# Setup of a graph-attention layer written into the layer's first units, and its residual formed on TensorE

## The reference, cut to what matters

```python
def _L0_gnn_ref(inputs, adj, W, a, bias, res_w, res_b):
    h = inputs @ W
    hr = h.reshape(N, F_OUT, H)
    s_src = jnp.einsum('nfh,fh->nh', hr, a[:F_OUT])
    s_dst = jnp.einsum('nfh,fh->nh', hr, a[F_OUT:])
    e = s_src[:, None, :] + s_dst[None, :, :]
    e = jnp.where(e >= 0, e, ALPHA * e)
    att = jax.nn.softmax(e * adj[:, :, None], axis=1)
    out = jnp.einsum('ijh,jfh->ihf', att, hr)
    out = out.reshape(N, H * F_OUT)
    out = out + bias
    out = out + inputs @ res_w + res_b
    return out
...
x = _layernorm(x + _L0_gnn_ref(x, adj, ...), axis=-1)
x = _layernorm(x + _L1_gnn_ref(x, adj, ...), axis=-1)
```

## Time and profile before

| | |
|---|---|
| median of 3 runs | 4077.73 us |
| profiled execution | 4075.24 us |
| its span in the profile | 4073.3 us |
| first `ex` of layer 0 starts | 137.03 us |
| last `ex` of layer 0 starts | 1542.88 us |
| TensorE, VectorE, ScalarE busy (share of the span) | 90%, 88%, 75% |

### The profile page before, as it was taken

How to read it: one execution, slowest core, us unless ns; L and a number is a source line. 1 busy time by engine, 2 the same in 40 slices (tenths; PEclk the granted TensorE clock), 3 DMA queues, 4 the chain that set the end, 5 groups by cost and what they waited for, 6 DMA issues and landing times.

```text
span 4073.3 us, 66286 instructions
## 1 busy us (share of the span) xinstructions
PE 3664.9 (90%) x25304; PEld 3075.6 (76%) x25304; DVE 3599.6 (88%) x6302; ACT 3068.7 (75%) x3075; POOL 1336.9 (33%) x1508
## 2 busy tenths in 40 slices
PE   7688888888888886999999979999999999999994
PEld 5577777777777774788787858888888788888883
DVE  2899999999999995999999779999999899999994
ACT  3699999899899985555555458888888788888870
POOL 0000000000000000111111035555555469999996
PEclk8899999999999997999999999999999999999997
DMA  3211121121121114000000142333333333333331
GB/s 111 98 54 54 60 74 54 54 79 55 54 72 62 54 54 129 19 17 19 18 17 21 28 142 90 101 101 102 102 102 101 117 111 114 117 117 116 116 109 40
DMA packets 160174, 311.37 MB, mean 76 GB/s; under 512 B 17642, under 2 KB 122346, under 8 KB 155346
## 3 DMA queue, kind: packets, MB, share of 16 engines
q1 hardware_dynamic: 159826, 306.88, 23.1%
HBM read 260.87 MB, written 45.94 MB: 75 GB/s over the span
## 4 chain that ended last, share of the span: by engine, by line
ACT 32%; POOL 20%; DVE 17%; PE 15%; issue 14%; DMA 1%; DVEq 0%; SPq 0%; ACTq 0%; POOLq 0%; PEldq 0%; PEld 0%
ACT b L1008 8%; PE ps L791 7%; ACT b L1144 6%; ACT b L1145 6%; ACT b L1001 5%; DVE b L1349 4%; DVE b L1516 3%; POOL b L585 2%; DVE b L1407 2%; POOL b L582 2%; DVE b L1405 2%; PE ps L747 2%; ACT b L1125 2%; PE ps L932 2%; POOL b L579 2%
## 5 line engine op out<-in xcount | busy, mean ns | idle before, releaser
L859 PE MATMUL ps<-b 128*128 128x257 f32 x4096 | 911.2, 382 | 20.7 <-DMA b<-in_adjTb 11.7
L932 PE MATMUL ps<-b 128*128 128x257 f32 x4096 | 903.0, 380 | 0.0
L859 PEld LDWEIGHTS ps<-b 128*128 128x128 f32 x4096 | 776.8, 190 | 146.1 <-DMA b<-in_adjTb 12.7
L932 PEld LDWEIGHTS ps<-b 128*128 128x128 f32 x4096 | 772.0, 190 | 113.4 <-ACT b L1082 0.8
L791 PE MATMUL ps<-cb,b 128*128 128x128 f32 x4096 | 566.3, 298 | 250.5 <-ACT b L1001 236.9
L791 PEld LDWEIGHTS ps<-cb,b 128*128 128x128 f32 x4096 | 506.3, 154 | 303.6 <-ACT b L1001 245.5
L1296 DVE SCALAR_TENSOR_TENSOR b<-b 128x4096 f32<-128x4096 f32 x128 | 566.5, 4425 | 60.9 <-ACT b L995 58.3
L1298 DVE CUSTOM_DVE_ANT_0 b<-b 128x4096 f32<-128x4096 f32 x128 | 566.4, 4425 | 5.4 <-DMA b<-in_adj 1.0
L548 POOL TENSOR_TENSOR cb<-cb 128x1 f32<-128x1 f32 x32 | 39.4, 1230 | 1521.9 <-DVE cb L1282 1521.9
L1008 ACT ACTIVATE b<-ps 128x1024 f32<-128x1024 f32 x512 | 493.6, 1023 | 45.9 <-PE ps L791 45.5
L747 PE MATMUL ps<-b 128*64 128x128 f32 x8192 | 510.3, 276 | 0.0
(11 more groups left out here) (192 smaller groups left out, 4877.6 us busy)
## 6 DMA issues: line engine op xcount, KB each, us to landing
b<-in_adjTb SPq DMA_DIRECT2D x256, 512.0 KB, 3.7
b<-in_adj SPq DMA_DIRECT2D x32, 2048.0 KB, 8.3
y_d<-b SPq DMA_DIRECT2D x64, 128.0 KB, 1.8
h_d<-b SPq DMA_DIRECT2D x64, 128.0 KB, 1.8
b<-h_d SPq DMA_DIRECT2D x64, 128.0 KB, 2.5
b<-in_xT SPq DMA_DIRECT2D x1, 4096.0 KB, 16.4
b<-in_x SPq DMA_DIRECT2D x32, 128.0 KB, 2.1
b<-y_d SPq DMA_DIRECT2D x32, 128.0 KB, 2.0
```

Source lines behind the costliest of these rows:

```text
L859: last = mm(b[:, 0:XA], aj[:, q % AJR, e, :], xf[:, j, :], start=(j == 0), stop=(j == NT - 1))
L932: last = mm(o[:, 0:XA], at[:, q % ATR, b, :], xa[:, j, :], start=(j == 0), stop=(j == NT - 1))
```

## The change

The ring `pt` has 4 buffers where it had 5; the buffers of the setup are laid over buffers that layer 0 uses later (xT over the second adjacency buffer and `pt`, `hr` over `ub[2]`). The barrier `kA` is gone, and each user waits for the semaphore of what it needs. xT is loaded in four quarters, each with a semaphore of its own, and the adjacency of tile 0 right behind. ScalarE's and TensorE's setup steps are interleaved: two tiles of features follow each broadcast from the fifth on (`groups`), and `linear(0)`, `linear(1)`, `ex(0)`, `ex(1)` and `linear(2)` stand between them.

The x @ res_w tile, its bias sum on VectorE and the tensor `y0_d` are gone. VectorE adds the identity to res_w once, so that x @ (res_w + I) is residual and input together, and adds the two biases once. In `turn_back(t)` TensorE forms identity x bias plus x @ (res_w + I) for the tile in the upper half of the PSUM bank; SyncE loads the tile's columns of xT for it (`xtl`). ScalarE copies the result to `ys` in a new step `ev_y0`, behind `ex` of the units with h = 1, and `post_a` waits for that copy.

```diff
-    PTR = 5
+    PTR = 4
...
+        groups = {i: (2 * (i - NL // 2) + 1, 2 * (i - NL // 2) + 2) for i in range(NL // 2, 2 * NL)}
+        groups[2 * NL] = tuple(range(3 * NL + 1, NT))
...
-            ld(xT_s, xT.rearrange("(k p) n -> p k n", p=128), s_x0)
+            for q in range(4):
+                w = slice(q * N // 4, (q + 1) * N // 4)
+                ld(xT_s[:, :, w], xT[:, w].rearrange("(k p) n -> p k n", p=128), s_x0[q])
...
-                    ld(ys[:, r % 2, :], tile_of(y0_d, r), s_y0l[r % 2])
+                    if r >= 1:
+                        sp.wait_ge(s_of, r)
+                    ld(xtl, xT[:, r * 128:(r + 1) * 128].rearrange("(k p) n -> p k n", p=128), s_xtl)
...
             def turn_back(t):
                 pe.wait_ge(s_ot, t + 1)
+                pe.wait_ge(s_xtl, 16 * (t + 1))
+                y = bank(6 + t % 2)[:, 256:512]
+                mm(y, ident_s, bb, start=True, stop=False)
+                for k in range(2):
+                    mm(y, xtl[:, k, :], RW[:, k, :], start=False, stop=(k == 1))
...
+            def ev_y0(t):
+                ac.wait_ge(s_of, t + 1)
+                if t >= 2:
+                    ac.wait_ge(s_t, xslot[t - 2] + 1)
+                    ac.wait_ge(s_yd[t % 2], 16 * (t // 2))
+                act(ys[:, t % 2, :], bank(6 + t % 2)[:, 256:512], ACT.Copy).then_inc(s_yv, 1)
...
-            linear(0)
-            linear(1)
+            features_ev(0)
+            for i in range(NL // 2):
+                broadcast_ev(i)
+            linear(0)
...
+            for i in range(NL // 2, 2 * NL):
+                broadcast_ev(i)
+                for t in groups[i]:
+                    features_ev(t)
+                if i == NL - 1:
+                    linear(1)
+                if i == NL + 2:
+                    ex(0)
+                if i == 2 * NL - 1:
+                    ex(1)
+                    linear(2)
+            for t in groups[2 * NL]:
+                features_ev(t)
             for u in range(NU):
-                ex(u)
+                if u >= 2:
+                    ex(u)
+                if u % 4 == 1 and u >= 5:
+                    ev_y0(u // 4 - 1)
...
             def post_a(t):
-                ve.wait_ge(s_of, t + 1)
-                ve.wait_ge(s_y0l[t % 2], 16 * (t // 2 + 1))
+                ve.wait_ge(s_yv, t + 1)
```

More of the change, by code:

```diff
@@ L132, in gat_topp_kernel @@
         WD = p0.take(2, 40)
[L133 to L138, removed]
+        bb2 = p0.take(256)
         w1s = p0.take(256)
@@ L231, in gat_topp_kernel @@
         s_c = sem("s_c")
-        s_x0 = sem("s_x0")
-        s_xi = [sem(f"s_xi{i}") for i in range(4)]
-        s_y0 = [sem(f"s_y0{i}") for i in range(4)]
+        s_x0 = [sem(f"s_x0{i}") for i in range(4)]
+        s_rw = sem("s_rw")
+        s_bb = sem("s_bb")
+        s_rwi = sem("s_rwi")
+        s_xtl = sem("s_xtl")
+        s_gw = sem("s_gw")
+        s_mc = sem("s_mc")
+        s_yv = sem("s_yv")
         s_ms = sem("s_ms")
@@ L250, in gat_topp_kernel @@
         s_adj = [sem(f"s_adj{i}") for i in range(2)]
-        s_y0l = [sem(f"s_y0l{i}") for i in range(2)]
         s_gu = sem("s_gu")
@@ L348, in _ @@
[L348 to L351, removed]
+            ld(adj_s[0], tile_of(adj, 0), s_adj[0])
+            ld(ident_s, ident, s_rw)
+            ld(RW, res_w.rearrange("(k p) n -> p k n", p=128), s_rw)
+            ld(bb, bias.partition_broadcast(128), s_rw)
+            ld(bb2, res_b.partition_broadcast(128), s_rw)
@@ L699, in _ @@
             last.then_inc(s_wa, 1)
[L700 to L704, removed]
             pe.wait_ge(s_wab, 1)
-            pe.wait_ge(s_x0, 16)
             for c in range(NL):
+                pe.wait_ge(s_x0[4 * c // NL], 16)
                 if c >= 2:
@@ L713, in _, with broadcast @@
                 last.then_inc(s_sr, 1)
-            pe.wait_ge(s_lo, NL)
-            pe.wait_ge(s_sel, 1)
-            for i in range(2 * NL):
+            def broadcast(i):
                 h, c = divmod(i, NL // 2)
@@ L723, in _, with features @@
                 last.then_inc(s_sd, 1)
-            pe.wait_ge(s_sdc, 2 * NL)
-            for t in range(NT):
+            def features(t):
                 if t >= 2:
                     pe.wait_ge(s_hc, 2 * (t - 1))
-                    pe.wait_ge(s_yo, 2 * (t - 2) + 1)
                 for k in range(2):
[L730 to L733, removed]
+                    last = mm(bank(5 + t % 2)[:, 0:264], xT_s[:, k, t * 128:(t + 1) * 128], WA[:, k, :],
                               start=(k == 0), stop=(k == 1))
                 last.then_inc(s_pm, 1)
-            barrier(pe, kA)
+            features(0)
+            pe.wait_ge(s_lo, NL)
+            pe.wait_ge(s_sel, 1)
+            for i in range(NL // 2):
+                broadcast(i)
+            pe.wait_ge(s_w1, 16 * 2)
+            for k in range(2):
+                last = mm(bank(7)[:, k * 64:(k + 1) * 64], w1s[0:64, k * 128:(k + 1) * 128], w2s[0:64, :],
+                          start=True, stop=True)
+            last.then_inc(s_m, 1)
+            for i in range(NL // 2, 2 * NL):
+                broadcast(i)
+                for t in groups[i]:
+                    features(t)
+            for t in groups[2 * NL]:
+                features(t)
+            pe.wait_ge(s_hc, 2 * NT)
+            pe.wait_ge(s_rw, 16 * 4)
+            pe.wait_ge(s_rwi, 1)
+            pe.wait_ge(s_gw, 16)
+            pe.wait_ge(s_mc, 1)
             def pv(gq):
@@ L1052, in _ @@
             out_turned(NT - 1)
+            ev_y0(NT - 1)
             ev_x(NT - 1)
@@ L1257, in _ @@
                                 ALU.subtract).then_inc(s_lo, 1)
[L1258 to L1264, removed]
-                v.tensor_tensor(yo[:, t % 4, :], yo[:, t % 4, :], bb[:, 0, :], ALU.add).then_inc(s_yo, 1)
-            barrier(ve, kA)
+            ve.wait_ge(s_rw, 16 * 4)
+            v.tensor_tensor(bb, bb, bb2, ALU.add).then_inc(s_bb, 1)
+            for k in range(2):
+                c = slice(128 * k, 128 * k + 128)
+                last = v.tensor_tensor(RW[:, k, c], RW[:, k, c], ident_s, ALU.add)
+            last.then_inc(s_rwi, 1)
             def post_a(t):
-                ve.wait_ge(s_of, t + 1)
-                ve.wait_ge(s_y0l[t % 2], 16 * (t // 2 + 1))
+                ve.wait_ge(s_yv, t + 1)
                 z = 4 * (t % 4)
```

94 lines of the change are left out of this document (50 added, 44 removed).

## The result

The changed kernel takes 4187.25 us (median of 4 runs, 4183.44 to 4191.52) against 4078.03 us, a ratio of 1.0269 with a 95% interval of 1.0251 to 1.0286. It is 109 us slower; the forecast was 74 us, with a range up to 4205.

What follows compares the result with a forecast made beforehand. It took the ring ScalarE-TensorE-ScalarE to bound layer 0, with VectorE close behind. Setup -65, ring and residual +107, tail +2 and clock +30 gave +74 us, 4152 us, range 4105 to 4205.

Steps and rivals of the forecast that it cites:

- The ring of 4 buffers: Fourth eviction waits for pv(g0-1): 1.02 us longer per unit with h = 2 and 3, no cost with h = 0.
- The rival in which the ring does not bind: Products released before the fourth eviction asks; only ev_y0 (31 times 0.4 us) and the tail remain: 4027 us, chance 0.07.
- The unit with h = 1: Three residual products delay TensorE's first transposes by 1.29 us; with the ring's wait the unit gets 1.36 us longer.
- The residual's price: Three products of 256 columns per tile on TensorE take 1.29 us; copy ev_y0, some 0.4 us, is free while the ring waits.
- VectorE's new wait: post_a stands behind ev_y0 and starts near 550.6 instead of 547.9; no cost, row maximum ends before the ex needing it.
- The clock: TensorE's gaps grow to about 3.05 us, bringing more slow transpose starts at 1.66 us each: +30 us, bounds 0 and 96.
- My bound of +96: Clock's upper case, all 93 gaps followed by slow starts, 58 more; as a rival 4218 us, chance of more than +60 0.12.
- The setup: Earlier start and interleaved groups bring ex(2) from 158.24 to 93.4 us: -65 us, bounds -50 and -75.
- The tail: At layer 0's end turn_back(31) and ev_y0(31) stand in an uncovered chain: 1.3 + 0.5, +2 us.
- The sum: Whole kernel: -65 + 107 + 2 + 30 = +74 us, 4152 us on the median of the runs.

Runs made afterwards that it cites:

- e5: Kernel before with a ring of 4 buffers and 16 extra transposes filling TensorE's gaps in units with h = 0, 2 and 3; 4107.23 us, ratio 1.0073.
- e6: Kernel before (ring of 5) with 8 extra transposes filling the same TensorE gaps; 4018.05 us, ratio 0.9853.
- e1: Kernel before with one edit, the ring pt at 4 buffers instead of 5; 4298.21 us, ratio 1.0545.
- e2: Changed kernel with the ring of 5 back, space taken from layer 1's weights U1, whose two loads are left out; 4033.86 us, ratio 0.9896.
- e12: Kernel before with a ring of 4 and all four products of a unit behind its four transposed chunks; 4017.48 us, ratio 0.9852.
- e4: Changed kernel with 16 extra transposes filling TensorE's gaps in units with h = 0, 2 and 3; 4089.96 us, ratio 1.003.
- e8: Changed kernel, ring of 4, with all four products of a unit behind its four transposed chunks; 4000.3 us, ratio 0.9811.
- e9: Kernel before, ring of 5, with all four products of a unit behind its four transposed chunks; 4016.19 us, ratio 0.9847.
- e11: Changed kernel with all four products behind the four chunks and TensorE's wait for U1 moved from unit 0 to unit 9; 3993.46 us, ratio 0.9793.
- e3: Changed kernel without the three residual products in turn_back, copy and waits kept; 27136.79 us, as other numbers set off layer 1's exact search.

## Why the prediction was right, and what was mis-sized

**The ring of 4 buffers** was the step that carried it, and it holds in the units with h = 0, 2 and 3. Predicted 1.02 us per unit with h = 2 and 3, measured 1.10 (9.69 to 10.79): the fourth eviction went on 1.20 us after the product's start (558.47 to 559.67), not 1.14. With the clock held up the ring alone costs 89 us (e5 against e6). In h = 0 it costs nothing, as predicted (12.36 and 12.37 us in warm units). The rival in which the ring does not bind is refuted by e1 and e2; e12 shows that it binds in this order on TensorE alone.

**The unit with h = 1** was mis-sized. I had 1.36 us, ring and residual together; it is 1.88. Of my 1.36 the three products were 1.29 and the ring 0.07. Measured apart they are 1.30 (e2) and 0.59 (e1), so the ring was the term that was too small. I had taken the 4.82 us from the first transpose to pv(g0-1) from a unit with h = 3. In the unit with h = 1 the fourth chunk waits for the first eviction, and the earlier trace rows have 550.15 and 555.42, 5.27 us; with it the ring comes to 0.52.

The residual's price was right in size and wrong in its path, which is luck. I followed the delay of TensorE only into the transposes and on to the ring's wait; for the rival without that wait I left 0.4 us per tile, the copy alone. But `ev_rows` waits for a product that stands behind the new ones as well, 1.04 us after `ev_y0`; then `linear` and the first eviction are late, ring or no ring. The copy is nearly free because ScalarE would wait for `ev_rows` in that time, and not because of the ring.

**VectorE's new wait** behind `ev_y0` (84.4 us in the window) costs nothing, as predicted: no `ex` waits for VectorE.

**The clock.** Predicted +30 us over the kernel before. From the rows: 33 starts at 1.6 us and 17 at 2.8 us more than a warm one make some 100 us, against 60 before (36 at 1.66): +41. e4 measures the 100 as 97, e6 the 60 as 59. The sign was right; two steps behind the size were not.

- I took the share of slow starts as a function of the gap's length. Behind the regular gaps of 1.0 to 1.7 us no start is slow (e4, e5, e6, e8, e9, e11, e12). But at one and the same length of 3.12 us I count, from 162 us on, 47 slow of 91 in the changed kernel and 85 of 90 in e1.
- I took 30 and not 60 because a slow start hardly ever followed another. In the changed kernel 18 of the 50 do, and 17 of those are of the long kind, all that it has. That kind is in no row of the kernel before except at the first start.

The three traces with this gap differ by the head of the unit: with h = 0 nearly all starts are slow in each (28, 28 and 30 of 31 in the changed kernel, e3 and e1), with h = 2 it is 4, 27 and 30. The unit ahead of the latter is the one with h = 1, 12.56, 11.41 and 11.26 us long. Each start that is slow shifts all later ones, so the pattern may lock onto itself; that is argued, not shown, and what decides is not settled here.

That the sum stayed in the range is thus partly luck. With the 60 short and 23 long slow starts of e3 in place of its own, the changed kernel would have taken some 60 us more, about 4247, outside the range (an estimate from the same 1.6 and 2.8 us). My bound of +96 would have been too low for e1, which lost 132 more than the kernel before.

**The setup.** Predicted -65, measured -56.7. The start of L705 at 10.63 us and the groups at about 2.6 us were within what I had taken. What I missed is the order of the loads: SyncE issues U1 only when all features are formed (83.27 us), and TensorE waits for it ahead of unit 0, 4.22 us at 87.46, and then starts slowly (32 transposes in 5.35 us, in e11 3.71). Without the load `ex(2)` starts 6.8 us earlier (e2), most of the 8.3 us that I was off. I had read the queue only for what stands behind `turn_back`. e11 shows that the wait can be saved.

**The tail**: +2 predicted, +3.6 measured.

**The sum** is then -56.7 + 31 tiles of 4.1 (127) + 2 + 41 + 3.6 + 1.6 = +118, against 115.5 between the profiled executions; here the 2 is the first tile's last units, and the 1.6 us are layer 1. Against the 74 of the forecast: 8 from the setup, 22 from the units, 11 from the clock, 3 from the end and layer 1.

So the change was three things in one. The setup between the first units gains 57 us. The residual on TensorE takes back about 40. The buffer given up for it cost some 147 us: 89 of wait (e5 against e6) and 58 of slow starts (97 us of them in the changed kernel, 24 at 1.6 us in e2). The 153 us between e2 and the changed kernel hold 6 or 7 us of the U1 load besides. The kernel before lost 21 us more to slow starts than e2 (59 against 38), and -57 + 40 + 147 - 21 is the measured 109. The buffer's cost follows from an order on TensorE that needed five buffers, and it goes with that order (e8, e12).

## What to carry to other kernels

A buffer taken from a ring is paid for by the wait that its count now names: look in the program order of the engine that frees it for what stands between, and reorder that before shrinking the ring. Read that path in each kind of unit by itself: 4.82 us in one was 5.27 us in the next, and the row was there. New waiting on TensorE can cost more than its own length through the clock: 89 us of waiting brought 132 us of slow starts in e1. Filling the gap with idle work is a cheap experiment that separates the wait from the clock; here the order that kept a unit's four products together shortened the gap to 1.69 us and removed both. A count of slow starts from one timing pattern should not be carried to another.

## What the runs showed of the hardware that was not expected

- With equal gaps of 3.12 us ahead of the same 24 transposes the slow starts were 50 of 125 in one kernel (after) and 91 of 125 in another (e1); leaving out three products per tile raised them to 83 of 125 and made the last `ex` of layer 0 start 21 us later (e3).
- There are two sizes of slow start: 4.2 to 4.5 us, and 5.38 us with a granted clock of 0.50 over the whole stretch. The long one appeared behind gaps of 3.12 us. In the kernels with shorter regular gaps it appeared only behind single gaps of 4.0 us (e12, unit 7) and of 22.6 us and more (unit 0). All 17 long starts of the changed kernel, all 23 of e3 and 29 of the 30 of e1 from unit 3 on stand directly behind another slow start.
- Some 1520 transposes of pure filling, about 1.9 us in each of 95 gaps, made the changed kernel 97 us faster (e4).
